# Early tile 0 of the expert product made earlier, and the slot table read before early tiles 3 to 5 are finished

## The reference

```python
def cond(x, weights, condition):             # x (64, 64, 1024), weights (16, 64, 64)
    return jnp.einsum('bct,bcd->bdt', x, weights[condition])
def ffn(x, W_gate, b_gate, W_e, b_e):        # 8 experts, W_e (8, 1024, 1024)
    logits = x @ W_gate + b_gate
    _, top_idx = jax.lax.top_k(logits, 2)
    y_all = relu(einsum('bsd,edh->bseh', x, W_e) + b_e)
    return take_along_axis(y_all, top_idx[..., None], axis=2).mean(axis=2)
out = x + ffn(cond(x, cond_weights, itok), W_gate, b_gate, W_e, b_e)
```

## Time and profile before

| what | value |
|---|---|
| device time, median of 3 | 883.5 us (883.22 to 887.41) |
| the profiled execution: time, span | 886.42 us, 884.7 us |
| PE busy | 851.7 us (96%) |
| POOL, DVE, ACT busy | 449.9, 422.4, 256.5 us |
| DMA, mean | 184 GB/s |
| TensorE clock granted, mean | 0.984 of full speed |

### The profile page before, as it was taken

How to read it: one execution, slowest core, us unless ns; L and a number is a source line. 1 busy time by engine, 2 the same in 40 slices (tenths; PEclk the granted TensorE clock), 3 DMA queues, 4 the chain that set the end, 5 groups by cost and what they waited for, 6 DMA issues and landing times.

```text
span 884.7 us, 16708 instructions
## 1 busy us (share of the span) xinstructions
PE 851.7 (96%) x4154; PEld 674.4 (76%) x4155; DVE 422.4 (48%) x595; ACT 256.5 (29%) x310; POOL 449.9 (51%) x500
## 2 busy tenths in 40 slices
PE   7898899999999999999999999999999999999993
PEld 4354478888888888888888888888888888888882
DVE  6697866836643273335533363336333733333320
ACT  5564512134421251114211331115111511112220
POOL 3002325366467667654665556555755565555311
PEclk9898999999999999999999999999999999999997
DMA  9999798998955695447754595547654664444433
GB/s 337 418 417 348 265 333 275 329 346 245 290 125 107 127 294 120 99 95 202 198 106 90 101 294 108 109 96 211 172 115 95 189 122 104 91 100 99 79 48 47
DMA packets 51034, 162.47 MB, mean 184 GB/s; under 512 B 11594, under 2 KB 11658, under 8 KB 50986
## 3 DMA queue, kind: packets, MB, share of 16 engines
q0 software_dynamic: 24544, 76.74, 40.3%
q1 hardware_dynamic: 20618, 67.79, 20.9%
q10 hardware_dynamic: 5840, 17.57, 5.1%
HBM read 106.74 MB, written 70.52 MB: 200 GB/s over the span
## 4 chain that ended last, share of the span: by engine, by line
PE 88%; DMA 4%; DVE 4%; issue 1%; ACT 1%; SPq 1%; POOL 0%; ACTq 0%; DVEq 0%; POOLq 0%
PE psO L607 85%; PE psO L548 2%; DMA y_rows<-ys 1%; DVE turned L855 1%; DMA first<-slot_table 1%; DMA slot_table<-lists 1%; DMA raw<-in_L_cond_weights 1%; ACT ys L700 1%; PE psG L560 1%; DVE w_lo L868 0%; SPq L325 0%; DVE place_hot L910 0%; DVE run_hot L918 0%; DVE idx_all L885 0%; POOL out L494 0%
## 5 line engine op out<-in xcount | busy, mean ns | idle before, releaser
L607 PE MATMUL psO<-w_hi,a_hi 128*128 (+1 forms) x1104 | 341.7, 391 | 0.2
L607 PE MATMUL psO<-w_lo,a_hi 128*128 (+1 forms) x1104 | 340.6, 390 | 0.0
L607 PE MATMUL psO<-w_hi,a_lo 128*128 (+1 forms) x1104 | 340.4, 389 | 0.0
L465 POOL DMA_INDIRECT rows<-y_rows,idx_g x248 | 260.6, 1051 | 106.7 <-issue 52.7
L607 PEld LDWEIGHTS psO<-w_hi,a_lo 128*128 128x128 f32 x1104 | 207.6, 188 | 43.3
L607 PEld LDWEIGHTS psO<-w_lo,a_hi 128*128 128x128 f32 x1104 | 207.7, 188 | 43.2
L607 PEld LDWEIGHTS psO<-w_hi,a_hi 128*128 128x128 f32 x1104 | 206.7, 188 | 44.4 <-issue 1.8
L1031 DVE TENSOR_TENSOR a_lo<-ys,a_hi 128x1024 fp32r<-128x1024 f32 x62 | 75.9, 1224 | 113.8 <-ACT a_hi L736 113.8
L724 ACT ACTIVATE ys<-ys 128x1024 f32<-128x1024 f32 x33 | 35.0, 1061 | 259.5 <-DVE ys L993 259.5
L724 ACT ACTIVATE rows<-rows 128x1024 f32<-128x1024 f32 x33 | 35.0, 1060 | 253.9 <-DVE rows L993 253.9
L993 DVE TENSOR_TENSOR ys<-psO,bias 128x1024 f32<-128x1024 f32 x33 | 40.3, 1222 | 125.4 <-PE psO L607 98.9
(11 more groups left out here) (141 smaller groups left out, 331.4 us busy)
## 6 DMA issues: line engine op xcount, KB each, us to landing
raw<-in_L_ffn_W_e SPq DMA_DIRECT2D x56, 512.0 KB, 6.0
y_rows<-ys ACTq DMA_DIRECT2D x32, 512.0 KB, 8.3
out<-in_x SPq DMA_DIRECT2D x14, 1024.0 KB, 9.7
rows<-in_x SPq DMA_DIRECT2D x16, 512.0 KB, 11.8
more_x<-in_x SPq DMA_DIRECT2D x16, 512.0 KB, 11.1
bias<-in_L_ffn_b_e SPq DMA_DIRECT2D x8, 512.0 KB
rows<-y_rows,idx_g POOLq DMA_INDIRECT x248
raw<-in_L_ffn_W_e POOLq DMA_DIRECT2D x4, 512.0 KB, 8.7
```

The lines of the kernel that those rows point to most:

```text
L465: pool.indirect_dma_start(out=rows[:, slot, a * DQ:(a + 1) * DQ], out_offset=None, in_=y_parts[0:(1 + TOK) * Q, :], in_offset=bass.Indirec ...
L607: last = nc.tensor.matmul(ps[:, h * BANK:(h + 1) * BANK], a[:, p, k * P:(k + 1) * P], w[:, bass.ds(slot + (k * H + h * BANK), BANK)], star ...
```

## The change

Early tile 0 is transposed into a buffer of its own, `early_f`, so it need no longer wait for the last chunk's split. On DVE `turn_early(0)` moves from behind token tile 28 to behind tile 24, and `early_lo(0)` from ahead of tile 29's transpose to behind tile 25's; on ACT `early_hi(0)` moves from behind tile 28's `y_out` to behind tile 24's. In DVE's loop `read_from` now stands behind `choose` and `turn_tokens` of its tile, not ahead of them. `fill(5)` leaves PE's token loop and becomes a hook of early tile 0, ahead of feature block 2. Behind the loop, `turn_early(1)` and `early_lo(1)` come ahead of `slots(6)`. Then ACT waits for the whole slot table and reads it back ahead of `early_hi(4)` and `relu` of tile 2, and DVE's index work comes ahead of `finish_early(3)`, `turn_early(5)`, `early_lo(5)` and `early_out(4, EARLY)`.

```diff
+            early_f = lend("early_f", [P, D])
-        FILL = {G * g + 11: g for g in range(NG - 2)}
+        FILL = {G * g + 11: g for g in range(NG - 3)}
-                early_products(0, hooks={3: lambda: ranks(NG - 2), 4: lambda: gate(NG - 1, 1, 0),
+                early_products(0, hooks={2: lambda: fill(NG - 3), 3: lambda: ranks(NG - 2), 4: lambda: gate(NG - 1, 1, 0),
                                          5: lambda: gate(NG - 1, 1, 1), 7: lambda: unstack(NG - 1)})
...
-                    nc.scalar.copy(a_hi[:, t % 2, :], early_t).then_inc(s_ahi, 1)
+                    nc.scalar.copy(a_hi[:, t % 2, :], early_t if t else early_f[:, :]).then_inc(s_ahi, 1)
...
-                    if n == NTILE - 4:
+                    if n == NTILE - 8:
                         early_hi(0)
...
                 early_hi(3)
-                early_hi(4)
-                relu(tile(0, 2))
                 for g in range(NG):
                     act.wait_ge(s_sc[g], LAND)
                 act.wait_ge(s_yout[0], 16 * NG)
...
                 for q in range(Q):
                     act.dma_start(ys[q * R:(q + 1) * R, 0, :].rearrange("p (b w) -> p b w", w=P).bitcast(U32),
                                   slots_all).then_inc(s_tab, 16)
+                early_hi(4)
+                relu(tile(0, 2))
                 relu(tile(0, 3))
...
-                    if t:
+                    if t == 1:
+                        dve.wait_ge(s_split, KD)
+                    if t > 1:
                         dve.wait_ge(s_alo, t)
-                    else:
-                        dve.wait_ge(s_split, KD)
...
                 for n in range(NTILE):
...
-                    if n == NTILE - 3:
-                        early_lo(0)
-                    if n in FROM:
-                        read_from(FROM[n])
                     if n in UNSTACK:
                         choose(UNSTACK[n])
                     turn_tokens(n)
+                    if n in FROM:
+                        read_from(FROM[n])
+                    if n == NTILE - 7:
+                        early_lo(0)
...
-                    if n == NTILE - 4:
+                    if n == NTILE - 8:
                         turn_early(0)
+                turn_early(1)
                 list_out(NG - 3)
+                early_lo(1)
                 slots(NG - 2)
-                turn_early(1)
-                early_lo(1)
                 choose(NG - 1)
...
                 read_from(6)
                 schedule()
-                early_out(4, EARLY)
-                finish_early(3)
-                turn_early(5)
-                early_lo(5)
...
                 to_out(idx_row[:, :], ys[:, 1, 0:COLS], ys[:, 1, COLS:2 * COLS])
                 dve.sem_inc(s_idx, 1)
+                finish_early(3)
+                turn_early(5)
+                early_lo(5)
+                early_out(4, EARLY)
```

More of the change, by code:

```diff
@@ L1004, in turn_early @@
                     dve.wait_ge(s_yx[t % 2], (t // 2 + 1) * (Q * 16))
-                    if t:
+                    if t == 1:
+                        dve.wait_ge(s_split, KD)
+                    if t > 1:
                         dve.wait_ge(s_alo, t)
-                    else:
-                        dve.wait_ge(s_split, KD)
-                    V.transpose(early_t.rearrange("p (k a i) -> p k a i", k=KD, a=Q),
+                    V.transpose((early_t if t else early_f[:, :]).rearrange("p (k a i) -> p k a i", k=KD, a=Q),
                                 fetched[t % 2].rearrange("p (a k j) -> p k a j", k=KD, a=Q)).then_inc(s_zt, 1)
@@ L1013, in early_lo @@
                     dve.wait_ge(s_ahi, t + 1)
-                    V.tensor_tensor(a_lo[:, t % 2, :], early_t, a_hi[:, t % 2, :], ALU.subtract).then_inc(s_alo, 1)
+                    V.tensor_tensor(a_lo[:, t % 2, :], early_t if t else early_f[:, :], a_hi[:, t % 2, :], ALU.subtract).then_inc(s_alo, 1)
                 def turn_rows(t):
```

## The result

The changed kernel took 887.94 us (median of 20 runs, 886.14 to 893.02) against 886.12 us of the kernel before (20 runs, 883.22 to 890.86): ratio 1.0025, 95% interval 1.0014 to 1.0037. It is slower by some 1.8 to 2.2 us, where 2.2 us less was forecast. The kernel before stood 2.6 us above the three runs that the prediction had for a base, so the forecast time missed by more than its reasons did.

A forecast was written before the change was run, and what follows sets the result against it. PE, busy 96% of the span, was taken as the bound. An earlier, full-clock early tile 0 gave 3.1 us, less 0.7 for a new pause and 0.2 for the table: 2.2 less, 881.3 us against 883.5; range 879.0 to 885.0.

The forecast's parts named there:

- read_from behind the transpose: DVE's token loop: `choose(3)` no longer waits 2.30 us; tile 19's transpose moves from 74.87 to 72.2, tile 24's to 87.0.
- turn_early(0) there: DVE behind tile 24: rows landed by 88.5; tile 25's transpose 0.8 us late, group 6's gate 1.5 late at 103.5.
- the displaced `y_out(25)`: ACT: `y_out(25)` comes only behind `early_hi(0)`, ends at 91.85, and tile 25's transpose on DVE starts 0.8 us late.
- PE from there: PE from group 6's gate to early tile 0: 6.9 us instead of 10.15, so early tile 0 starts at 110.4, 1.8 earlier.
- 1.7 us for full clock at early tile 0: PE at early tile 0: with no idle time ahead it runs at 2.4 GHz and saves 1.7 us.
- A new pause of PE: PE around product 27: stands over 2 us twice, half clock on products 28 and 29, cost taken as 0.7 us.
- turn_early(1) ahead of slots(6): DVE behind the token loop: hidden, since `slots(6)` waits for a hook anyway; without cover 2.4 us of DVE.
- The table ahead of tiles 4 and 5: ACT's table read and DVE's index work: 1.9 us of room, 0.2 us of PE stall taken, bounds 0 and 1.5.
- POOL gathers tile 7 sooner, but PE doesn't wait there: POOL's gather of tile 7: index work done 6 us earlier lets it start sooner, worth nothing to PE.
- The rival with the chance of 0.15: ACT's wait ahead of `early_hi(4)`: table lands at 153.5, `early_lo(5)` 3.9 us late, 3.2 slower, 886.7; chance 0.15.

The follow-up runs named there:

- w_after: The changed kernel with expert 1's first four chunk loads issued ahead of the last two copies of x and expert 1's bias: 887.21 us, ratio 1.0023.
- yout_after: The changed kernel with `early_hi(0)` behind `y_out(25)` on ACT instead of ahead of it: 886.78 us, ratio 1.0015.
- after_again: The changed kernel measured again, nothing edited: 889.39 us, ratio 1.0039.
- front_only: The changed kernel with the table's read on ACT and the index work on DVE put back in their old order: 888.94 us, ratio 1.0030.
- bias_after: The changed kernel with expert 0's bias loaded at the turn of tile 28, ahead of `table_out(4)`: 884.72 us, ratio 0.9998.
- back_only: The kernel before with only the table's read and the index work moved ahead, as in the change: 885.97 us, ratio 0.9988.
- bias_before: The kernel before with expert 0's bias loaded at the turn of tile 28: 885.96 us, ratio 0.9998.
- three: The changed kernel with the edits of yout_after, bias_after and w_after together: 885.82 us, ratio 0.9992.
- three_front: The kernel of three with the table's read on ACT and the index work on DVE put back in their old order: 880.32 us, ratio 0.9937.
- three_dve: The kernel of three with only ACT's table read put back behind `early_hi(4)` and `relu` of tile 2: 881.91 us, ratio 0.9966.
- yout_bias: The changed kernel with the edits of yout_after and bias_after: 887.57 us, ratio 1.0007.
- from_only: The kernel before with only `read_from` moved behind `choose` and `turn_tokens`: 885.87 us, ratio 0.9998.
- front_yout_bias: The kernel of front_only with the edits of yout_after and bias_after: 882.98 us, ratio 0.9971.

## Why the prediction was wrong

The front itself was read rightly, and the forecast ended where it ended too soon: it counted the gain at early tile 0 and took it that "from early tile 0's first matmul at 112.19 us PE works through to the last tile".

- **read_from behind the transpose**: right. Tile 19's transpose came at 71.91, forecast 72.2; tile 24's at 86.78 for 87.0.
- **turn_early(0) there**: right in its times (88.27, 91.54, gate of group 6 at 103.25; forecast 88.5, 91.9, 103.5), wrong in where it was followed to. That DVE is 1.5 us late was carried on along PE alone. `list_out(4)` stands in the same list, SP's `table_out(4)` waits for it, and behind that, in SP's list, stand the bias of expert 0, the copies and expert 1's weights. This is the step that failed: the bias, 3.7 us later, put `finish_early(0)` 2.4 us behind, and loading it elsewhere took the loss back (0.9998). Of the 3.7 us DVE's late list is only 1.6, which the prediction could have followed; SP took the list up 0.7 later still, 1.9 are the pause of SP inside `table_out(4)`, which nothing in its rows announced, and 0.5 were made up behind it. Without the pause, in w_after, `finish_early(0)` was on time, and the 2.65 us at early tile 5 took the gain. How much of the loss over all runs is the list's and how much the pause's stays open. And the displaced `y_out(25)` was priced as the 1.5 us it made; keeping its place gives 1.9 at the gate.
- **PE from there**: 110.4 forecast, 111.06 came, with a pause of PE, ACT and SP together at 107.5 to 109.8 in between; without one, in yout_after, the same stretch took 6.32 us, against 6.9 reckoned. The 1.7 us for full clock at early tile 0 did not come in the profiled execution; full clock came in after_again and front_only, with starts at 113.04 and 112.87. Both came in w_after, whose lists up to there are the changed kernel's: early tile 0 at 110.50, at full clock, and `fill(7)` 2.7 us ahead of the kernel before (136.18). So the terms were right as mechanisms, and worth nothing to the whole, since PE waited later.
- **A new pause of PE**: right. The half clock took products 28 and 29 whole (5.40 for 3.9, 1.5 more) and used up the room ahead of the gate; its own cost at the gate was 0.2 us or less, for the gate's transpose on DVE ended only at 103.08. The rule of the Trainium skill's page "TensorE: Matmul & The Clock Gate", section "HAM oscillation — how this bites in real kernels", that bursts between waits each start slow, agrees with these rows, in the changed kernel twice over: on products 28 and 29 and at early tile 0. Other rows here do not follow it: early tile 0 of after_again and front_only ran at full clock behind the same pause, and the last section has a wait of 2.74 us with full clock behind it.
- **turn_early(1) ahead of slots(6)**: nothing in the runs speaks against "hidden"; it was not tried alone.
- **The table ahead of tiles 4 and 5**: 0.2 us taken of 0 to 1.5. The condition was right ("the table must have landed by 149.6") and its side wrong: ACT found it landed only at 152.46 in the changed kernel, and at 147.9 to 151.3 in the versions whose front is faster. In the change as made it cost nothing measurable beside the front (1.0030 without it, 1.0039 with it): it makes the 0.93 us at early tile 5, and without it the wait at tile 8 is longer (2.15 for 1.32). Where PE is early it costs 5.5 us. The rival with the chance of 0.15 had the mechanism.
- **"POOL gathers tile 7 sooner, but PE doesn't wait there"**: true of the gathers. Tile 8 waits for expert 1's weights, behind which `parts(8)` stands on ACT and DVE; before, `a_lo` of tile 8 ended at 205.76 and PE began at 206.25: 0.5 us of room, which no row of the prediction showed.

What stays open is that pause of PE, ACT and SP (DVE worked on): it is in the profiles of the changed kernel and of front_only, at 107.5 to 109.8, and of after_again, 2 us later, and in none of w_after, bias_after and yout_after. A packet of instructions is loaded within 1 to 3 us of it, but one is in the others too. It is some 1.5 us of the way to early tile 0 in those profiles, and 1.9 us of the way to the bias in the changed kernel; no run tells its cause. Open too is a wait of PE for an `a_lo` at 251.5 to 253.8 in back_only (0.76 us), front_only (0.96) and bias_before (2.09), far behind everything that these edits move.

## What to carry to other kernels

Where a timeline shows an engine without a gap, ask of each thing that it needs later by how much it comes ahead: here 0.5 us at tile 8 and 1.0 at early tile 2 (`a_lo` ready at 139.70, used at 140.73), so that a start won by 4.5 us gave nothing measurable until the loads and the table's read behind it were moved too. Follow a delay through every queue that holds something behind it, the DMA issuer's above all: a list that left 2.3 us late there, and a pause in its issues, delayed a bias whose load took 14 us to land. And look for work that is ready behind a wait for a DMA in an engine's list: the cast behind the table's read stood 7 us (146.2 to 153.16).

## What the runs showed of the hardware

A wait of PE can cost more than its length. In three, behind the wait of 5.48 us at early tile 5, the granted clock was half for some 6 us (stretches: busy and matmuls of PE, clock, DMA share, GB/s):

```profile
168.00:170.00 2.00, 0.00 (x0) 1.00 1.02 365
170.00:172.00 2.00, 0.00 (x0) 0.78 1.03 401
172.00:174.00 2.00, 0.64 (x2) 0.50 1.06 365
174.00:176.00 2.00, 2.00 (x6) 0.50 0.62 215
176.00:178.00 2.00, 2.00 (x6) 0.52 0.45 131
178.00:180.00 2.00, 2.00 (x10) 1.00 0.92 309
```

The last finish came 7.8 us behind that of three_front (872.53 and 864.76), with early tile 0 at the same time (107.55 and 107.53): 5.5 us of wait and 2.3 of clock. In three_dve the wait of 2.98 us cost some 5. Waits of 2.65 us (w_after, early tile 5), 2.81 (yout_bias, early tile 5), 2.00 (yout_after, tile 8) and 1.81 (from_only, tile 8) were followed by half clock too, with rows of two matmuls 0.85 us apart where 0.46 is usual. But waits of 1.43 and 1.88 us at early tile 2 and of 2.15 (front_only) and 2.74 (front_yout_bias) at tile 8 were not: the length of the wait alone does not tell. PE in yout_after, then in front_yout_bias:

```profile
204.95 0.72 PE L608 MATMUL psO<-w_hi,a_hi 128*128 x2 [2.00 <-DVE a_lo L1032]
...
206.29 1.05 PE L608 MATMUL psO<-w_hi,a_lo 128*128 x2
```

```profile
204.45 0.72 PE L609 MATMUL psO<-w_hi,a_hi 128*128 x2 [2.74 <-DVE a_lo L1033]
...
205.48 0.62 PE L609 MATMUL psO<-w_hi,a_lo 128*128 x2
```

And a load of 512 KB took 14.2 us from its issue to the end of the wait for it (117.77 to 131.99), in a stretch where the DMA engines' share was 0.99 (118 to 132 us).
